# VectorE copies the values, ScalarE doesn't; an expert's weights are loaded in thirds: one change to a fused convolution, attention and expert kernel

## The reference

```python
x = x + conv(gn(x))                # 1x1 convolution over 192 channels and 28 correlations with near pixels
t = to_tokens(x)                   # (8 images, 256 tokens, 192)
t = t + attn(ln(t))                # one head, causal: softmax(q k^T / sqrt(192)) v
t = t + ffn(ln(t))                 # 8 experts, the best one per token

# ffn
gate = xf @ Wg.T + bg
vals, idx = top_k(gate, 1)         # softmax over one value is 1
h = silu(xf @ W1[idx].T) * (xf @ W2[idx].T)       # 469 wide
out = h @ W3[idx].T
```

## Time and profile before

| | |
|---|---|
| device time, median of 3 runs | 234.52 us (233.04 to 238.59) |
| the profiled execution | 233.54 us, its span 231.7 us |
| TensorE busy | 209.1 us (90%) |
| VectorE busy | 171.4 us (74%) |
| ScalarE busy | 113.9 us (49%) |
| GpSimd busy | 105.3 us (45%) |
| chain that ended last | PE 59%, DVE 16%, POOL 6%, issue 6%, DMA 6%, ACT 5% |

### The profile page before, as it was taken

The page is one execution under the profiler, slowest core; times in us unless marked ns, Lnnn a source line. Parts: engine busy times, 40 slices in busy tenths (PEclk is TensorE's granted clock), DMA queues, the critical chain, the costliest instruction groups (busy, mean ns, idle before and its releaser), DMA issues.

```text
span 231.7 us, 4547 instructions
## 1 busy us (share of the span) xinstructions
PE 209.1 (90%) x1331; PEld 182.4 (79%) x1331; DVE 171.4 (74%) x559; ACT 113.9 (49%) x244; POOL 105.3 (45%) x133
## 2 busy tenths in 40 slices
PE   6999799989899969998888799999999999999950
PEld 3686588968799958887665688898999999999940
DVE  3577897768399769699877789997767686868640
ACT  2276585175499697996640134343343333343410
POOL 4245756545439996896665103223131313131221
PEclk9999999999999999999999999999999999999995
DMA  6992247665730663647212332332001000000000
GB/s 218 366 350 87 83 126 187 170 219 165 252 135 0 237 234 117 221 188 259 81 52 63 80 86 70 93 83 78 21 14 37 17 34 20 34 17 22 33 20 0
DMA packets 16343, 26.46 MB, mean 114 GB/s; under 512 B 3795, under 2 KB 12673, under 8 KB 15424
## 3 DMA queue, kind: packets, MB, share of 16 engines
q1 hardware_dynamic: 14448, 22.65, 30.7%
q0 software_dynamic: 1872, 3.52, 4.4%
HBM read 19.76 MB, written 6.76 MB: 114 GB/s over the span
## 4 chain that ended last, share of the span: by engine, by line
PE 59%; DVE 16%; POOL 6%; issue 6%; DMA 6%; ACT 5%; POOLq 1%; DVEq 0%; ACTq 0%
PE bank L1468 8%; PE bank L1146 4%; PE bank L1333 4%; PE bank L1150 4%; PE bank L1149 4%; PE bank L1148 4%; PE bank L1147 4%; PE bank L1429 4%; PE bank L1469 3%; DMA stage<-in_w_all 2%; PE bank L1446 2%; PE bank L1192 2%; DMA taps_sb<-near_rows 2%; DMA out_rows<-yo,rows 1%; PE bank L1141 1%
## 5 line engine op out<-in xcount | busy, mean ns | idle before, releaser
L498 POOL DMA_INDIRECT out_rows<-yo,rows x23 | 23.2, 1011 | 76.9 <-DVE yo L1107 61.5
L1468 PE MATMUL bank<-wall,HH 128*128 (+1 forms) x88 | 28.1, 374 | 0.3 <-issue 0.3
L667 ACT ACTIVATE HH<-bank 128x512 fp32r<-128x512 f32 x23 | 13.8, 599 | 27.8 <-PE bank L1429 27.7
L1089 DVE TENSOR_TENSOR gh<-gh,bank 128x470 f32<-128x470 f32 x23 | 14.8, 645 | 14.5 <-PE bank L1150 14.4
L673 ACT ACTIVATE FH<-bank 128x256 fp32r<-128x256 f32 x23 | 8.9, 385 | 27.5 <-PE bank L1446 27.5
L1469 PE MATMUL bank<-wall,HL 128*128 (+1 forms) x88 | 22.1, 251 | 0.0
L1146 PE MATMUL bank<-wall,FH 128*128 (+1 forms) x46 | 19.3, 419 | 1.6 <-DVE FL L1092 1.6
L464 POOL DMA_INDIRECT token_rows<-rows,posi x16 | 16.9, 1055 | 7.3 <-issue 4.0
L670 ACT ACTIVATE gh<-bank 128x470 f32<-128x470 f32 x23 | 13.0, 565 | 13.1 <-PE bank L1150 13.1
L1278 PE MATMUL bank<-mH 128*128 128x512 f32 x73 | 19.3, 400 | 0.0
L1084 DVE TENSOR_TENSOR HL<-bank,HH 128x512 fp32r<-128x512 f32 x23 | 15.9, 691 | 3.6 <-ACT HH L667 3.4
(11 more groups left out here) (247 smaller groups left out, 647.4 us busy)
## 6 DMA issues: line engine op xcount, KB each, us to landing
stage<-in_w_all SPq DMA_DIRECT2D x7, 1324.0 KB, 5.7
rows<-token_rows SPq DMA_DIRECT2D x23, 98.0 KB, 2.0
near_rows<-gram SPq DMA_DIRECT2D x8, 243.0 KB, 3.2
xcm<-in_x_cm SPq DMA_DIRECT2D x2, 768.0 KB, 8.3
rows<-in_x_tm SPq DMA_DIRECT2D x1, 1536.0 KB, 14.0
stage<-in_w_all SPq DMA_DIRECT2D x4, 331.0 KB, 4.0
token_rows<-emptyt SPq DMA_DIRECT2D x3, 294.0 KB, 4.2
taps_sb<-near_rows SPq DMA_DIRECT2D x8, 103.0 KB, 2.1
```

The costliest lines, as they stand in the source:

```text
L498: pool.indirect_dma_start(out=out, out_offset=bass.IndirectOffsetOnAxis(ap=rows[:, j, C + 2:C + 3].bitcast(U32), axis=0), in_=yo[:, par], ...
L1468: nc.tensor.matmul(dst[:, 0:2 * C], HH[:, 1 - par, k], w(0, P, c0, c0 + 2 * C), start=(k == 0), stop=False)
```

## The change

ScalarE's `take_v` becomes VectorE's, with one multiply for both halves instead of two scaled copies. It stands behind `leftover` and ahead of `positions`, and for image 0 behind `leftover(0)`. An expert's weights are loaded by three transfers with a semaphore each; the first may start when GpSimd's L434 of expert e-2 is done, the second after `leftover`, the third after L437. `low_weights` pieces are dealt out anew. `taps` is filled first and TensorE waits for it alone, with six matmuls instead of three; five fills instead of eight stand in slot 0.

```diff
-            def weights_in(e):
-                sp.dma_start(stage[:, e % 2], w_all[e]).then_inc(stage_in[e % 2], 16)
+            def weights_in(e, part):
+                c = PARTS[part]
+                sp.dma_start(stage[:, e % 2, c], w_all[e][:, c]).then_inc(stage_in[e % 2][part], 16)
...
-            weights_in(1)
+            for part in range(3):
+                weights_in(1, part)
 
             for e in range(2, EXPERTS):
+                sp.wait_ge(wall_lo_a, e - 1)
+                weights_in(e, 0)
+                sp.wait_ge(wall_q, e - 1)
+                weights_in(e, 1)
                 sp.wait_ge(wall_lo, e - 1)
-                sp.wait_ge(wall_q, e - 1)
-                weights_in(e)
+                weights_in(e, 2)
...
+            nc.gpsimd.memset(taps[:].rearrange("p b h c -> p (b h c)"), 1.0).then_inc(filled, 1)
             nc.gpsimd.memset(half_c[:], -0.5).then_inc(filled, 1)
             nc.gpsimd.memset(emptyt[:], 0.0).then_inc(filled, 1)
             nc.gpsimd.memset(gram[:].rearrange("p b h c -> p (b h c)"), 0.0).then_inc(filled, 1)
-            nc.gpsimd.memset(taps[:].rearrange("p b h c -> p (b h c)"), 1.0).then_inc(filled, 1)
...
-                nc.gpsimd.tensor_tensor(w[:, W12:2 * W12], raw[:, 0:W12], w[:, 0:W12].bitcast(F32), ALU.subtract)
+                nc.gpsimd.tensor_tensor(w[:, W12:2 * W12], raw[:, 0:W12], w[:, 0:W12].bitcast(F32), ALU.subtract).then_inc(wall_lo_a, 1)
...
-            def take_v(t, par):
-
-                sc.wait_ge(v_ready, t + 1 + AHEAD)
-                v = bank[2][:, 0:HALVES * VW].rearrange("p (h c) -> p h c", h=HALVES)
-                nc.scalar.activation(V[:, par], v[:, :, EXPERTS:VW], ACT.Copy)
-                for h in range(HALVES):
-                    j = 2 * t + h
-                    ins = nc.scalar.activation(rows_all[:, j, 0:EXPERTS], v[:, h, 0:EXPERTS], ACT.Copy, scale=ln1s[:, j:j + 1])
-                ins.then_inc(v_copied, 1)
...
+            def take_v(t, par):
+
+                ve.wait_ge(v_ready, t + 1 + AHEAD)
+                v = bank[2][:, 0:HALVES * VW].rearrange("p (h c) -> p h c", h=HALVES)
+                at = slice(HALVES * t, HALVES * (t + 1))
+                nc.vector.tensor_copy(V[:, par], v[:, :, EXPERTS:VW])
+                scale = ln1s[:, at].rearrange("p (h a) -> p h a", a=1).to_broadcast([P, HALVES, EXPERTS])
+                nc.vector.tensor_tensor(rows_all[:, at, 0:EXPERTS], v[:, :, 0:EXPERTS], scale, ALU.mult).then_inc(v_copied, 1)
...
                 if 2 <= t <= SPLIT_LAST:
                     leftover(t - 1)
+                if on(t, 0):
+                    take_v(t, par)
                 if t in gate_of:
                     positions(gate_of[t], link)
...
                 if j == -1:
                     ffn_step(j, 1, False, False, True)
                     table_slots()
+                    low_weights(EXPERTS - 2, (4,))
                 elif j == 0:
                     ffn_step(j, 0, False, True, False)
                     norm_slot(1, 1, 1)
+                    low_weights(EXPERTS - 2, (5,))
                     ffn_step(j, 0, False, False, True, 2)
...
-                if 0 <= j < 3:
+                if 0 <= j < 2:
                     low_weights(EXPERTS - 2, (2 * j, 2 * j + 1))
-                elif 3 <= j < 6:
-                    low_weights(EXPERTS - 1, (2 * j - 6, 2 * j - 5))
+                elif 2 <= j < 6:
+                    low_weights(EXPERTS - 1, ((0, 1), (2, 3), (4,), (5,))[j - 2])
...
-            pe.wait_ge(filled, 4)
-            keep_busy(3, taps[:].rearrange("p b h c -> p (b h c)"))
+            pe.wait_ge(filled, 1)
+            keep_busy(6, taps[:].rearrange("p b h c -> p (b h c)"))
...
                 if j == 0:
-                    fill(8)
+                    fill(5)
```

More of the change, by code:

```diff
@@ L242, in build @@
         cm_in = [sem(f"cm_in{g}") for g in range(len(GANGS))]
-        stage_in = [sem("stage_in0"), sem("stage_in1")]
+        first_in = sem("first_in")
+        stage_in = [[sem(f"stage_in{par}{part}") for part in range(3)] for par in range(2)]
+        wall_lo_a = sem("wall_lo_a")
+        PARTS = (slice(0, W12), slice(W12, 2 * W12), slice(2 * W12, STAGE))
         empty_out = sem("empty_out")
@@ L329, in _ @@
                     c = slice(n * (b - 2), n * (b - 1))
-                    sp.dma_start(stage[:, 0, c], w_all[0][:, c]).then_inc(stage_in[0], 16)
+                    sp.dma_start(stage[:, 0, c], w_all[0][:, c]).then_inc(first_in, 16)
                 if 4 <= b < 4 + HEAD_PARTS:
@@ L374, in _ @@
             nc.gpsimd.memset(gram[:].rearrange("p b h c -> p (b h c)"), 0.0).then_inc(filled, 1)
-            nc.gpsimd.memset(taps[:].rearrange("p b h c -> p (b h c)"), 1.0).then_inc(filled, 1)
-            pool.wait_ge(filled, 2)
+            pool.wait_ge(filled, 3)
             nc.gpsimd.iota(emptyt[:, C + 2:C + 3].bitcast(I32), pattern=[[0, 1]], base=NO_TOKEN, channel_multiplier=0).then_inc(empty_ready, 1)
@@ L546, in weights_hi @@
                     sc.wait_ge(conv_taken, IMAGES)
-                sc.wait_ge(stage_in[e % 2], 16 * (e // 2 + (1 if e % 2 else FIRST_PARTS)))
+                if e == 0:
+                    sc.wait_ge(first_in, 16 * FIRST_PARTS)
+                else:
+                    sc.wait_ge(stage_in[e % 2][part], 16 * ((e + 1) // 2))
                 if part == 0:
@@ L596, in step @@
                     norm_image(t)
-                if on(t, 0):
-                    take_v(t, par)
                 if 1 <= t < EXPERTS:
@@ L640, in _ @@
                     weights_hi(2, 0)
-                if i == IMAGES + 2:
-                    take_v(0, 0)
                 if i == 1:
@@ L760, in take_gram @@
                 ve.wait_ge(rn_ready, b + 1)
-                ve.wait_ge(filled, 3)
+                ve.wait_ge(filled, 4)
                 if b >= 2:
@@ L812, in low_weights @@
                 raw3 = raw[:, 2 * W12:STAGE].rearrange("p (k c) -> p k c", c=C)
+                ve.wait_ge(wall_hi, e + 1)
+                ve.wait_ge(wall_hiq, e + 1)
+                ve.wait_ge(wall_hi3, e + 1)
+                ve.wait_ge(wall_lo, e)
                 for n in pieces:
-                    if n == 0:
-                        ve.wait_ge(wall_hi, e + 1)
-                        ve.wait_ge(wall_hiq, e + 1)
-                        ve.wait_ge(wall_hi3, e + 1)
-                        ve.wait_ge(wall_lo, e)
                     if n < 2:
@@ L1007, in _ @@
                     leftover(0)
+                    take_v(0, 0)
                 if i == IMAGES + 3:
```

## The result

The kernel after takes 235.87 us, median of 20 runs (234.90 to 237.30), against 233.98 us for the kernel before (20 runs, 231.85 to 238.59). The ratio is 1.0123 with an interval of 1.0101 to 1.0144: a small loss, clear of noise, and inside the two per cent. The ratio compares fast executions alone (those not over 1.5% above the fastest of their kernel), while the two medians take in all and are 0.8% apart. The profiled execution has a span of 233.5 us against 231.7.

What follows compares the result with a forecast made beforehand. TensorE was taken to bound the expert stage, whichever other engine is last each attention step. From the profiled 233.54 us, +3.0 attention, -0.8 expert stage and 0 head gave 235.7, range 232.0 to 237.3.

Steps and rivals of the forecast that it cites:

- A: Main case: the gate and `leftover` on VectorE both stand behind GpSimd instructions in attention step 4; 235.7 us, chance 0.42.
- Step 1: Attention stage: `take_v(1)` waits for the last matmul of the values, so L776 starts at 65.6, 1.2 us late.
- XL(2): XL(t) is the start of VectorE's first `low_xt` instruction in attention step t; for t = 2 forecast at 68.6 us.
- Steps 2 to 4: Attention stage: `leftover` stands behind GpSimd, the 1.80 load wait goes, step 4 has two meetings; XL(5) 2.9 us late.
- Step 5: Attention step bound by ScalarE, which no longer copies the values: 0.3 us shorter.
- Steps 6 and 7: Attention stage: step 6 +0.6 for `take_v` and -0.2 at the gate; in step 7 TensorE's counts hide most of `take_v`.
- Head: Kernel start: six calls on the taps, half of them fast, end at 7.6; term 0, ends -0.9 and +2.4 us.
- E: Slower rival, at the kernel's start: the clock's level rises only after the six calls; 238.5 us, chance 0.07.
- B: Rival: only one meeting, as `leftover` in attention step 4 is issued just ahead of L434; 234.2 us, chance 0.18.
- C: Rival: no meetings in the attention stage, the gate's L850 slips past L437; 233.0 us, chance 0.22.
- D: Faster rival: step 1's delay is absorbed and the load's 1.8 kept; 230.9 us, 230.0 with the head's best, chance 0.11.
- F: Rival on the loads in thirds: they bring nothing since ScalarE never waits long for a load; no chance given.

## Why the prediction was right, and where it was not

The time was forecast as 235.7, with a range of 232.0 to 237.3; it is 235.87. The case is A, two meetings. But two terms were missing or wrong, and they are of the size of what was forecast.

**Step 1: right.** L776 (now L773) was put at 65.6 and stands at 65.32; XL(2) at 68.6, and it is 68.33. Against XL(1) that is +1.16, the forecast 1.2. Half of it is the order: `take_v` waits 0.54 us for the last matmul of the values, and everything behind it waits too. The other half is the copy itself, 0.57 (64.75 to 65.32), and 0.53 of step 1 stayed when the copy was moved behind the statistics. The price of `take_v` was 0.6 and is 0.69 (75.31 - 74.63, its start to the next instruction's), within its bounds.

**Steps 2 to 4: right, mechanism and size.** XL(3), XL(4), XL(5) were put at 75.7, 82.2 and 93.7, and are at 75.50, 81.97 and 93.29, with XL(1) 0.24 early. GpSimd's last third was put at 85.7 to 87.5 and ran from 85.34 to 87.17; the first of the next expert at 88.5, and it began at 88.18. Step 4 lost 3.37 us (11.32 against 7.95): 1.00 at the gate, 1.43 at `leftover`, 0.69 by `take_v`, and 0.26 because the gate comes later behind XL(4) (below, step 6). The kernel with the bias in PSUM gets the 2.46 of the meetings back and keeps the rest. One size was off: GpSimd's L445 ended 1.19 us after the gate was issued and not 1.6, and the gate stood 1.0. It cost nothing in the sum, since the end of L442 decides when `leftover` is through; the gate's stand matters by putting `leftover` behind L442's start. The Trainium skill, page "SBUF — State Buffer", section "Who interferes with whom", says that a VectorE instruction with two SBUF inputs contends with a GpSimd instruction that reads SBUF, and that one with at most one doesn't, outside the modes that use both of its port pairs. The runs agree with both: two SBUF inputs stand (1.64, 2.02, 2.57, 3.14), one doesn't (0.62, issued 0.66 us into GpSimd's 1.84).

**Step 5: the step that failed.** The prediction said that step 5 is ScalarE's and gains 0.3; it lost 0.78. The prediction followed the late XL(5) through VectorE and stopped there. Late next is TensorE: its five fills run out at 91.74 (90.42 + 1.32), and it has nothing to do until XL(5) is through, at 94.20. The cost is 1.03 us (7.51 against 6.48 with more fills). So a stall on another engine was costed at its own length only, while TensorE's fills covered only the length it had before. Step 5 without the fall gained 0.25, as forecast.

**Steps 6 and 7.** Forecast +0.4, measured +0.69 and +0.23. The gate does not stand at 104.81 (0.64), as said, but it comes 4.01 us behind XL(6) and not 3.75 (104.81 - 100.80, against 101.23 - 97.47 before). It comes as late in the kernel with the values alone (102.31 - 98.30), so it belongs to them. TensorE's last transpose of the turned image, before and after, and the gate after, show why:

```profile
96.19 0.27 PE L1260 MATMUL bank<-small_sb,xn 128*64 128x128 f32 x1
```

```profile
99.78 0.27 PE L1270 MATMUL bank<-small_sb,xn 128*64 128x128 f32 x1
104.81 0.64 DVE L855 SCALAR_TENSOR_TENSOR bank<-rows,small_sb 128x8 f32<-128x8 f32 x4
```

From that transpose to the gate it is 5.04 us before (96.19 to 101.23) and 5.03 after; only XL(6), in between, has moved forward, from 1.28 behind the transpose to 1.02. Behind the transposes TensorE goes through the scores, five fills and the projection nearly without a gap, and ScalarE's `take_u`, VectorE's `low_u` and the gate follow the projection. So the 0.26 that ScalarE's relief gains in a step is given back in the next one if that has a gate. The sum counted the gain and not its return. The three terms of step 6 are 0.66 for `take_v` (its price in step 4 of the kernel with the values alone), 0.26 for this, and -0.23 for the gate's shorter instructions: 0.69. The +0.23 behind XL(7) is in the kernel with the values alone too (21.51), and where it comes from isn't shown.

**Expert stage: right.** -1.07 against -0.8, inside 0 and -1.3. The five fills run from 135.63 for 1.32, and the transposes follow at 137.04. The part alone shows 1.06. How it divides between the fills and the pieces wasn't tried.

**Head: wrong in its size.** The sum had 0, with a rise of the clock after half of the six calls. The six calls' length came out right (6.4 forecast, 6.28 in the mean), but TensorE started at 1.84 and not at 1.2, in all eight profiles, although the taps were filled by 1.13 in the kernel after; what it waited for isn't shown. And the credit of 0.7 for faster sums behind was read off, where 1.36 lies between the first three calls and the next five. That was an execution with a late rise. In three of the other profiles with the old head the eight matmuls take 1.03, in one 0.97 and in one 1.25, so there is little to gain in the usual case. One execution's draw was taken for the rule. The bounds (-0.9 to +2.4) held it. E, all six slow, did not occur, though 7.17 is not far from its 8.4. (TensorE's wait there is at L1335, not L1338 as named ahead of the prediction.)

**How it came out right.** The ratio gives 2.9 us (2.4 to 3.4, 0.0101 and 0.0144 of 233.98); the two medians are 1.89 apart. By stretches it is +4.49 in attention, -1.07 in the expert stage, +0.97 for the head's mean and -1.4 behind the last `yo`: 3.0. The forecast had +2.2, less than the ratio's interval and more than the two medians have between them. It was 1.2 short in the two stages (1.03 of it the clock's fall) and 1.0 short at the head, and it knew nothing of the 1.4 at the end, which took most of that back. That the time came out within 0.2 us of 235.87 is luck: errors of opposite sign cancelled.

**The rivals.** B (the gate stands, `leftover` doesn't) was not seen in any profile; the reverse was, in the two with step 1 moved. C (none) is what the kernel with the bias in PSUM shows: 0.997, or 233.3, with both meetings of step 4 gone; C had said 233.0. D (faster) had step 1 absorbed and the load's 1.8 kept. Neither happens: step 1 is late by its 1.16, and even with the thirds alone, where it isn't delayed at all, the load's gain is lost at the gate. F was right in its outcome, but for another reason: the load's gain is not hidden, it is eaten.

## What to carry to other kernels

Before an engine is relieved, ask what its neighbours then meet. Here three edits that each removed a real wait (a full ScalarE, a late load, a late first fill) lost 0.9 to 1.7% alone. The early load brought the instructions behind it onto GpSimd's; the values made VectorE's work longer in steps 2, 4 and 6, where it is late, and put a wait into step 1; the early fills took six calls where three had done. In the kernel after, moving one small operand to PSUM was worth 1.5%, and with it the same thirds became a gain.

Stalls of the neighbours have a second price at TensorE. Where fills keep its clock up, they are counted for the idle time of the kernel in which they were put there; a stall that is a microsecond longer needs more of them.

A single profiled execution shows one draw of the things that vary. For the head and for the end of the program it takes several profiles of kernels with the same part to see the mean.

## What the runs showed of the hardware

**The clock.** In the attention stage idle times of TensorE of 1.68, 1.69, 1.79, 2.45, 3.03 and 3.05 us were each followed, within 2 us of its return, by a granted clock of 0.50. In the kernel before it stood for 1.52 us and kept 1.00. Each fall cost about 1 us of the step (0.9 to 1.4), and 2.8 in the longest. But no single number separates the cases. The kernel with the thirds alone fell after standing for 1.26 us, and the kernel after with the values on ScalarE kept 1.00 at the same place after 1.25; the kernel before kept it after two microseconds (82 to 84) in which TensorE was busy for 0.48. With an unchanged attention stage the kernels with only the pieces and only the head fell in step 4, where the kernel before did not in its one profile. On what a fall depends beyond the idle time is open.

**An instruction load at the end.** The time from the last `yo` to the end is 6.1 to 6.2 us in five profiles and 7.5 to 7.9 in nine. In all nine, and in none of the five, one packet of 0.02 MB on the queue for instructions moves at about the time of the last but one scatter of the output. The DMA queues of the kernel before in the 7 us around its last `yo`, and the wait for that scatter in its chain:

```profile
q0 software_dynamic: 66, 0.01, 0.9%
q8 instruction: 1, 0.02, 0.8%
```

```profile
222.86 3.44 DMA out_rows<-yo,rows
```

In the kernel after there is no line for instructions in that stretch, and the scatter takes 2.06 us:

```profile
q0 software_dynamic: 96, 0.00, 0.8%
```

```profile
226.01 2.06 DMA out_rows<-yo,rows
```

The scatter has to land before the last one is issued, so 1.4 us of it are at the end of the path. The Trainium skill, page "Runtime: NRT & Kernel Launch", section "Instruction fetch mechanics", says that engines fetch their instructions in blocks over a DMA queue of their own, and that a block's cost is mostly hidden. Here the scatter beside which such a packet moves takes 3.40 to 3.90 us, and 2.06 to 2.12 without one, so 1.3 to 1.8 us are not hidden. That the packet is the cause is inferred from these fourteen profiles; nothing was changed to test it. All kernels without the new pieces have it there, five of the ten with them do, too. Whether that is fixed by a program's length or changes from one execution to the next is open: there is one profile of each. It may be part of the reason why the pieces alone gained 1.3% and not the 0.45% of their stretch.
